# When ScalarE casts the routed rows: step 13 or step 6 of an odd phase

## The reference

```python
x = x + tanh(g_xattn[0]) * attention(layernorm(x), ctx, ctx, encoding, Wq, bq, ...)
x = x + tanh(g_ffn[0]) * routed_moe(layernorm(x), gate_w, w0, w1, wo)

# attention: 16 heads of 16, over n = 512
q, k, v = W @ input + bias;  q, k = rotary(q), rotary(k)
prob = softmax(q^T k / 4);  out = Wm @ (prob applied to v) + bm

# routed_moe: 8 experts, the two best for each token
logits = x @ gate_w;  top 2;  weights = softmax(top logits)
out = sum over e of cw[:, e] * (silu(x @ w0[e]) * (x @ w1[e])) @ wo[e]
```

## Time and profile before

| | |
|---|---|
| median of 3 runs | 1193.34 us (1193.08 to 1194.62) |
| the profiled execution, its own time | 1194.62 us |
| its span | 1192.7 us |
| PE busy | 1092.7 us (92%) |
| DVE busy | 803.6 us (67%) |
| ACT busy | 686.9 us (58%) |
| POOL busy | 383.5 us (32%) |

### The profile page before, as it was taken

The page is one execution under the profiler, slowest core; times in us unless marked ns, Lnnn a source line. Parts: engine busy times, 40 slices in busy tenths (PEclk is TensorE's granted clock), DMA queues, the critical chain, the costliest instruction groups (busy, mean ns, idle before and its releaser), DMA issues.

```text
span 1192.7 us, 17436 instructions
## 1 busy us (share of the span) xinstructions
PE 1092.7 (92%) x5417; PEld 439.7 (37%) x5417; DVE 803.6 (67%) x1585; ACT 686.9 (58%) x937; POOL 383.5 (32%) x492
## 2 busy tenths in 40 slices
PE   3788999989999999988749999999999999999996
PEld 1222333323333333323224444444444444444442
DVE  7778888978979787897365565656556573664631
ACT  2167777767777677787634465556447462653421
POOL 4473637666584837221220111101111111111101
PEclk8689999999999999999669999999999999999998
DMA  6326536242343313112448476767668675674333
GB/s 202 110 67 203 156 105 212 74 134 84 83 148 94 101 54 127 54 38 89 178 155 202 81 196 141 202 139 207 140 135 208 141 172 117 157 191 72 68 55 54
DMA packets 191383, 153.49 MB, mean 129 GB/s; under 512 B 131137, under 2 KB 152385, under 8 KB 191297
## 3 DMA queue, kind: packets, MB, share of 16 engines
q1 hardware_dynamic: 180640, 131.74, 39.2%
q0 software_dynamic: 7744, 18.09, 8.7%
q10 hardware_dynamic: 2912, 2.60, 0.7%
HBM read 73.67 MB, written 41.75 MB: 97 GB/s over the span
## 4 chain that ended last, share of the span: by engine, by line
PE 76%; DVE 10%; ACT 7%; issue 3%; DMA 2%; another core or an unknown queue 1%; POOL 0%; SPq 0%; DVEq 0%; ACTq 0%; POOLq 0%
PE psum L1209 32%; PE psum L1219 16%; PE psum L337 7%; PE psum L324 6%; ACT wh L483 6%; PE psum L221 5%; DVE MX L670 4%; PE psum L312 3%; PE psum L264 3%; PE psum L231 2%; PE psum L246 1%; ACT wh L433 1%; PE psum L282 1%; PE psum L252 1%
## 5 line engine op out<-in xcount | busy, mean ns | idle before, releaser
L1209 PE MATMUL psum<-wh,xT 128*128 128x512 f16 x1728 | 382.9, 382 | 13.0 <-DVEq L1352 11.0
L483 ACT ACTIVATE wh<-psum,es 128x512 f32<-128x512 f32 x512 | 321.8, 689 | 78.8 <-PE psum L324 71.8
L670 DVE TENSOR_REDUCE MX<-psum 128x2 f32<-128x1024 f32 x256 | 310.2, 1218 | 69.8 <-PE psum L312 63.7
L1209 PEld LDWEIGHTS psum<-wh,xT 128*128 128x128 f16 x1728 | 169.9, 98 | 220.0 <-issue 19.1
L1219 PE MATMUL psum<-wh,hT 128*128 128x512 f16 x864 | 194.1, 381 | 3.5 <-DMA hT<-hn 3.5
L324 PE MATMUL psum<-stg 50*128 50x512 f16 x512 | 146.7, 398 | 28.7 <-ACT wh L483 23.0
L1374 POOL DMA_INDIRECT out<-yb,target x36 | 56.5, 1568 | 339.0 <-ACT yb L1250 326.0
L1323 DVE TENSOR_TENSOR hh<-sg,psum 128x512 f32<-128x512 f32 x72 | 49.3, 685 | 156.8 <-ACT sg L1240 156.8
L337 PE MATMUL psum<-wh,vT 128*32 128x512 f32 x1024 | 144.4, 638 | 0.0
L548 ACT ACTIVATE wh<-stg,scw 128x1024 f16<-128x1024 f32 x96 | 102.6, 1137 | 46.1 <-DVE c L600 30.9
L555 DVE SCALAR_TENSOR_TENSOR wh<-stg,scw,wh 128x1024 f16<-128x1024 f32 x96 | 117.1, 1278 | 12.7 <-ACT wh L548 12.2
(11 more groups left out here) (197 smaller groups left out, 1035.4 us busy)
## 6 DMA issues: line engine op xcount, KB each, us to landing
stg<-in_w SPq DMA_DIRECT2D x16, 2048.0 KB, 10.2
stg<-in_wo SPq DMA_DIRECT2D x8, 2048.0 KB, 10.4
stg<-scr SPq DMA_DIRECT2D x186, 64.0 KB
Xs<-zero SPq DMA_DIRECT2D x40, 264.0 KB, 2.9
wh<-wh SPq DMA_DIRECT2D x64, 128.0 KB, 2.0
scr<-wh SPq DMA_DIRECT2D x32, 256.0 KB, 2.6
xs<-in_x SPq DMA_DIRECT2D x8, 512.0 KB, 4.6
out<-xs SPq DMA_DIRECT2D x8, 512.0 KB, 3.1
```

The lines of the kernel that those rows point to most:

```text
L483: act.activation(m.Pb[:, c % 2, hh, :], m.psT[tile % 2], ACT.Exp, scale=m.es[:, hb // 2:hb // 2 + 1]).then_inc(S["exped"], 1)
L670: dve.tensor_reduce(m.MX[:, hb % 2, c0:c0 + 9:8], m.psS[tile % 2], AX_X, ALU.max, negate=True).then_inc(S["maxed"], 1)
L1209: last = pe.matmul(m.psum[:, 2 * j + w, :], m.xT[:, 4 * xp + k, :], m.wh[(e % 2, w)][:, wp, c:c + 512], start=(k == 0 and xp == 0 and wp = ...
```

## The change

`rows_upper` is called at step 6 in every odd phase, where it was at step 13 in phases 3 to 15. Seven instructions of ScalarE move; the one of phase 17 was at step 6 and stays. Its waits move with it (for X2, and from batch 2 on for the transfers of two batches earlier). No other engine's instructions change their order.

```diff
-                if ph % 2 and 0 <= (ph - 3) // 2 < NB and s == (13 if ph < LAST else 6):
+                if ph % 2 and 0 <= (ph - 3) // 2 < NB and s == 6:
                     rows_upper((ph - 3) // 2)
```

## The result

The changed kernel is slower: 1199.76 us (median of 8 runs, 1195.22 to 1204.33) beside 1192.91 us for the kernel before (8 runs, 1189.02 to 1194.62), and the ratio on record is 1.0073 with the 95% interval 1.0046 to 1.0100. (These two medians alone give 1.0057; over all 17 runs of the changed kernel on record the median is 1201.04 us, which fits the higher ratio.) The direction was forecast and the size was not: 1197.0 us is 0.31% over the median given at the start, and 0.73% was measured, at least 0.46%. The median lies within the range, near its upper end at 1200.0. Two later measurements put the ratio at 1.0101 [1.0074, 1.0129] and 1.0094 [1.0059, 1.0129]. So there are 7 to 13 us to explain where 3.7 had been worked out.

The account below looks back on a forecast made before the run. TensorE holds 76% of the chain; ScalarE reaches it through two score banks. Additions of 4.7 us at step 6 less 1.0 at step 13 give 3.7 us: 1197.0 us against the median 1193.34, range 1193.0 to 1200.0.

Parts of the forecast that it names:

- The push of one cast: Step 6: the cast delays step 7's exponentials and so TensorE's logits by 0.93 us, in full in phases 5, 11, 13, 15.
- TensorE's new wait: Sign in the profile: TensorE waits 0.7 to 0.9 us for ScalarE before step 8's second flipped tile, seven times.
- VectorE's cover in phases 3, 7 and 9: Before the k projection, VectorE being late hides part of the push, leaving 0.44, 0.44 and 0.12 us.
- The removal: Step 13 without the cast gives back 0.5 us each in phases 11 and 13, 0 elsewhere: 1.0 us.
- The work in all: Whole kernel: additions of 4.7 us at step 6 less 1.0 us gained at step 13, 3.7 us slower.
- new dips in phases 3, 7, 9 and 13: New gaps at step 8 bring clock dips of 1.7 us each to these phases: 1202.4 us, chance 0.04.
- more: Rival, chance 0.13: all seven phases pay 0.93 us with nothing back, 1199.8 us, or new clock dips, 1202.4 us.
- Seven full pushes: Part of a rival: no VectorE cover, seven phases pay 0.93 us, nothing returns: +6.5, 1199.8 us; rival's chance 0.13, clock part 0.04.
- GpSimd in phase 13: L613 runs early beside VectorE's L677, stretching it to 1.6 us; hidden by 0.1 us, else at most 1.6 us.

Follow-up runs that it names:

- null: The kernel before, unchanged, run and profiled again: 1183.92 us beside 1184.71, ratio 0.9996.
- null2: The kernel before, unchanged, run once more on another chip for its profile: 1185.65 us beside 1185.87, ratio 0.9994.
- rem: The kernel before with the cast at step 13 cut to 8 columns in phases 7 to 15: 1189.11 us beside 1190.95, ratio 0.9991.
- s8: The kernel before with the casts of phases 3 to 15 moved from step 13 to step 8: 1187.52 us beside 1184.71, ratio 1.0018.
- again: The changed kernel, unchanged, measured again: 1197.79 us beside 1184.71 for the kernel before, ratio 1.0101.
- again2: The changed kernel, unchanged, measured once more: 1196.37 us beside 1185.87 for the kernel before, ratio 1.0094.
- add2: The kernel before with a second cast at step 6 of phases 3 to 15, second measurement: 1197.19 us beside 1185.87, ratio 1.0090.
- fill: The changed kernel with three 512-column matmuls per odd phase in TensorE's waits at step 8: 1196.79 us beside 1190.95 for the kernel before, ratio 1.0050.
- fill2: Same kernel as fill, the changed kernel with three added matmuls at step 8, second measurement: 1192.32 us beside 1185.87 for the kernel before, ratio 1.0053.
- mid: The kernel before with two 496-column matmuls added between the halves of the logits, phases 3 to 15: 1197.55 us beside 1190.95, ratio 1.0055.
- half: The kernel before with the casts of phases 3 to 15 split, half at step 6, half at step 8: 1196.47 us beside 1190.95, ratio 1.0050.
- add: The kernel before with a second cast at step 6 of phases 3 to 15, first measurement: 1194.27 us beside 1184.71, ratio 1.0063.

## Why the prediction was too small

**The push of one cast: right.** At the full clock the stretch from step 1 to step 9 is 14.95 us without the cast at step 6 (seven phases of null, null2, rem and s8) and 15.90 with it (five of again, again2 and add2): 0.95 for 0.93. Summed over phases 3 to 15 and less the lost clock, that stretch is 103.6 to 104.5 us in null, null2, rem, s8 and before, and 109.5 to 110.4 in the changed kernel, add2, fill and fill2: about 6, seven times 0.93 being 6.5. TensorE's new wait comes in two parts, of 0.41 and 0.19 us, where one of 0.7 to 0.9 had been forecast.

**VectorE's cover in phases 3, 7 and 9: wrong.** Forecast 0.44, 0.44 and 0.12 us. Measured 0.95 in phases 3 and 9, and by add2's rows as much in phase 7. In the one profile VectorE reached the logits of phase 9 0.70 us after their end, and in phase 3 0.28 us; in null's phase 9 and in null2's phase 3 it was waiting for them (0.24 and 0.48 us). A sum from one execution took scatter for slack. It is worth 1.9 us.

**The removal: right in phases 11 and 13, too small elsewhere.** 0.51 in phase 11, and in phase 13 15.1 us from step 9 on with the cast at 13 (mid), 14.6 without (half, fill). But phase 3, for which nothing was counted, gives back 0.51 too (the bound had been 0.5), and phase 5 0.18 (17.48 us in again, 17.66 in add2).

**The work in all: near, with errors that partly cancel.** 4.7 + 1.9 - 1.0 - 0.7 = 4.9 us, where 3.7 had been worked out; the rest of the changed kernel grew by 3.4 and 2.8 (0.9 and 0.8). For add and add2, with nothing given back, 6.6 is to be expected and the rest grew by 6.7 and 3.8 (0.9 and 1.1).

**The clock: the step that failed.** The prediction gave new dips in phases 3, 7, 9 and 13 a chance of 0.04 as the second half of the rival "more", with 1202.4 us, and put it at nothing in the sum. It argued that the dips fell in phases whose logits came without a wait, and that phase 3 with its wait of 0.72 us stayed at 1.00. Both came from one execution. That wait stands behind the logits and not before them, and the dips of before wander: phases 5 and 11 in its first profile, 3, 5, 7, 11 and 13 in null, 5 to 13 in null2. What was read as a property of the phase was one throw. In the odd phases 3 to 15 lost clock is 11.6, 17.0 and 17.0 us in three profiles of before, and 24.5, 23.6 and 22.2 in three of the changed kernel; the longer dip in phase 13 is about a third of that difference. Over all runs of the two later measurements it is 8 to 10 us more, two to three times the rest's share, and with the new waits filled most of it is gone. So the rival's mechanism is the likeliest reading for the larger part, with the limits named under fill. The Trainium skill ("TensorE: Matmul & The Clock Gate", section "A second HAM failure mode: psum-queue depth-cycling") says that frequent micro-idles between groups of matmuls make the clock swing. These runs agree in direction, with new waits of mostly 0.41 and 0.19 us in each of seven phases and 9 us more of lost clock, and the prediction was wrong to hold one profile against it.

**"Seven full pushes", 1199.8 us,** hit the measured median by chance: nothing given back and no clock. The seven pushes are there in full, but the removal gives back, and the clock makes up for that.

**GpSimd in phase 13: wrong.** L613 was to run beside L677 from step 7. In the changed kernel:

```profile
500.84 0.38 POOL L561 PARTITION_ALL_REDUCE mxa<-mxr  x1 [6.09 <-issue]
508.43 2.12 POOL L613 TENSOR_TENSOR Xr<-X,Xr 128x1024 f16<-128x1024 f32 x1 [7.21 <-issue]
```

The cast had ended at 505.05, and L677 came and went in 0.17 us at 505.59. L613 starts 7.3 to 7.6 us after this reduction's start in all three profiles of the changed kernel, with no releaser shown. The reduction may hold GpSimd far longer than the recorded 0.38 us; no run tested it. L613 never met L677, so the 1.6 us at stake there were not paid. Whether its early run has to do with the longer dip of this phase is open.

**Open.** Why a given phase dips in one execution and not in the next. Why phase 13 dips longer without the cast at step 13. Why half of the push (half) has two thirds of the lost clock, and why s8 and mid, with no new wait before the logits, have +4.1 (1.7) and +4.0 (2.0): these are too near to each other's errors. What makes the 9.1 us of stalls in even phases. They don't belong to the change: the same sum is 98.7 to 101.7 us in mid, rem, half and fill, which ran on one chip, and 93 to 94 in null, s8, again, null2, again2, fill2 and add2, which ran on two others.

## What to carry to other kernels

Work out a push from the timetable, as here, but read the clock over several executions before arguing from where its dips fall: one profile shows one throw. A cover read from one execution deserves the same doubt: VectorE's lateness of 0.3 to 0.7 us was gone in the next. Where an edit puts a new wait of even half a microsecond on TensorE, price the clock beside the wait; here lost clock was the larger part. An insertion on a helper engine belongs where that engine waits for TensorE anyway: two steps later the same cast was free within 0.4%.

## What was not expected of the hardware

Adding matmuls whose results nobody reads made a kernel faster: 1192.32 against 1196.37 us on the same chip, with 7.7 us (2.6) less lost clock and 3.1 (0.9) more of the rest. And the mean granted clock differs between executions of one kernel by enough to move a single span by several microseconds: the changed kernel's runs on one chip lie between 1192.06 and 1203.64 us, those of before between 1178.73 and 1188.17.
